# Feed-forward phases: one ring of three PSUM banks for both kinds of centred tiles, a new order in each queue, no loop

## What is computed

```python
def _qlinear(x, W, b):
    y = q_acc(jnp.einsum('bsk,nk->bsn', q_mul(x), q_mul(W)))   # q_mul: fp8 e5m2, q_acc: fp16
    return q_acc(y + q_mul(b))
h = jax.nn.relu(_qlinear(x, W1, b1))      # 24 -> 96
y = _qlinear(h, W2, b2)                   # 96 -> 24
...
t = t + ffn(_ln_t(t), ...)                # _ln_t: (v - mean) / sqrt(var + 1e-5) over channels
x = x + next_mixer(_ln_c(x))              # _ln_c: the same with 1e-6
```

## Time and profile before

| what | value |
|---|---|
| median of three runs | 3313.1 us |
| the profiled execution | 3312.0 us, span 3310.4 us |
| granted TensorE clock, mean | 0.969 |
| TensorE busy | 2831.6 us (86%) |
| VectorE busy | 2666.6 us (81%) |
| ScalarE busy | 2258.8 us (68%) |
| GpSimd busy | 1860.7 us (56%) |
| feed-forward of layer 0 | about 462 to 632 us of the span |
| of layer 1 | 1971 to 2146 us |
| of layer 2 | 2676 to 2851 us |
| of layer 3 (last) | 3165 to 3310 us |

### The profile page before, as it was taken

One profiled execution on the slowest core, in us unless ns is written; L12 is line 12 of the kernel. 1 busy time (PEld: TensorE's weight loads), 2 busy tenths in 40 slices (PEclk: granted clock), 3 DMA queues, 4 the chain that ended last, 5 costly groups with the idle time before them and its releaser, 6 DMA issues. The chain is left out here.

```text
span 3310.4 us, 65685 instructions
## 1 busy us (share of the span) xinstructions
PE 2831.6 (86%) x20846; PEld 1477.4 (45%) x20846; DVE 2666.6 (81%) x4380; ACT 2258.8 (68%) x4205; POOL 1860.7 (56%) x1466
## 2 busy tenths in 40 slices
PE   8999989686999999999997678789999779688876
PEld 5666654233444444444442224344444334477732
DVE  6888879536999999999999958769999968444468
ACT  5666658576999898989895427666777558444455
POOL 2333323155889898989897635447777745100046
PEclk9999999898999999999999999989999989899999
DMA  2000001256474747474746232201101012301023
GB/s 88 0 0 0 0 14 45 81 172 175 120 209 135 221 140 222 140 217 141 217 124 185 59 79 74 76 21 25 24 23 25 18 56 89 126 22 23 22 71 78
DMA packets 201533, 294.28 MB, mean 89 GB/s; under 512 B 62242, under 2 KB 179158, under 8 KB 201110
## 3 DMA queue, kind: packets, MB, share of 16 engines
q1 hardware_dynamic: 198678, 288.03, 30.3%
q10 hardware_dynamic: 2688, 4.29, 0.4%
HBM read 190.11 MB, written 102.09 MB: 88 GB/s over the span
## 5 line engine op out<-in xcount | busy, mean ns | idle before, releaser
L1780 POOL TENSOR_TENSOR mam_hc<-mam_h,mam_cs 128x896 f32<-128x896 f32 x336 | 703.5, 2094 | 173.5 <-DVE mam_h L1699 98.7
L1699 DVE TENSOR_TENSOR_SCAN mam_h<-mam_a,mam_kept,mam_dbx 128x448 f32<-128x448 f32 x672 | 737.7, 1127 | 48.4 <-ACT mam_a L1569 47.4
L1422 PE MATMUL mam_ps_y<-mam_hc,mam_ident 128*128 128x448 f32 x1344 | 570.8, 558 | 124.8 <-POOL mam_hc L1780 124.7
L1569 ACT ACTIVATE mam_a<-mam_ft,mam_a_neg 128x448 f32<-128x448 f32 x672 | 409.5, 657 | 77.1 <-DVE mam_h L1699 76.0
L1422 PEld LDWEIGHTS mam_ps_y<-mam_hc,mam_ident 128*128 128x128 f32 x1344 | 249.8, 193 | 425.4 <-POOL mam_hc L1780 216.2
L1686 DVE TENSOR_TENSOR mam_dbx<-mam_ps_u,mam_bs 128x448 f32<-128x448 f32 x672 | 380.7, 610 | 0.0
L682 POOL TENSOR_TENSOR att_prob<-att_prob,att_share 128x588 f32<-128x588 f32 x128 | 149.0, 1186 | 306.8 <-DVE att_share L974 306.8
L2209 POOL TENSOR_TENSOR scan_ch<-scan_h,scan_cs 128x392 f32<-128x392 f32 x192 | 263.7, 1387 | 56.5 <-DVE scan_h L2150 55.3
L368 POOL MEMSET f_squares_ln<- 128x392 f32 x4 | 1.7, 424 | 362.5 <-POOLq L2283 326.5
L387 POOL CAST f_h<-f_hr 128x392 fp8e5<-128x392 f16 x128 | 65.3, 510 | 234.1 <-DVE f_hr L308 234.1
L2150 DVE TENSOR_TENSOR_SCAN scan_h<-scan_decay_by_column,scan_h,scan_drive_by_column 128x392 f32<-128x392 f32 x112 | 196.8, 1757 | 0.0
(11 more groups left out here) (240 smaller groups left out, 6631.1 us busy)
## 6 DMA issues: line engine op xcount, KB each, us to landing
mam_taps<-normed SPq DMA_DIRECT2D x220, 130.5 KB
mam_bs<-dram_bc SPq DMA_DIRECT2D x56, 448.0 KB, 9.1
mam_cs<-dram_bc SPq DMA_DIRECT2D x56, 448.0 KB, 11.7
normed<-f_staged SPq DMA_DIRECT2D x96, 203.0 KB
mam_ft<-dram_steps SPq DMA_DIRECT2D x42, 448.0 KB, 4.8
f_mixed<-mixed SPq DMA_DIRECT2D x64, 196.0 KB, 2.4
mam_gt<-dram_gs SPq DMA_DIRECT2D x48, 224.0 KB, 2.7
dram_gs<-mam_gs SPq DMA_DIRECT2D x47, 224.0 KB, 2.8
```

Source lines behind the costliest of these rows:

```text
L1422: mm = pe.matmul(ps_y[p % 2][:, 0:MT], ident[:], hc[t % 2][:, i, :], start=False, stop=(t % 8 == 7 and i == 1))
L1569: act.activation(a[t % 3][:, i, :], ft[p % 2][:, 0, :], ACT.Exp, scale=a_neg[:, at:at + 1]).then_inc(decays, 1)
L1699: dve.tensor_tensor_scan(h[:, n % 8, :], a[t % 3][:, i, :], dbx[:, i, 0:MT], kept[:, at:at + 1], ALU.mult, ALU.add).then_inc(scanned, 1)
L1780: pool.tensor_tensor(hc[t % 2][:], h[:, row:row + 2, :], cs[:, 2 * pair:2 * pair + 2, :], ALU.mult).then_inc(weighed, 1)
```

## The change

The three PSUM banks of centred tiles (two for ff, one for norm) become one ring of three; chunk c of either kind uses bank 2c mod 3. The norm of chunk c moves on VectorE from the end of slot c+3 to the middle of slot c+4 (lag 4). VectorE's slot is ordered by source: first the four steps that read PSUM (round_third, quantize, round_result, norm), then the five on SBUF. GpSimd's quantize_third(c) waits also for hidden8(c), that is for VectorE's cast of the same chunk, and its loop becomes quantize_third(c), update(c-1), add_mixed(c+4). TensorE's slot becomes second_product(s-2), subtract_mean(s+1), the norm's subtract_mean(s-3), variance(ff, s+1), hidden_units(s), variance(ln, s-3). ScalarE's becomes round_hidden(s-1), square(ff, s+1), square(ln, s-3), inverse_deviation(ff, s+1), inverse_deviation(ln, s-3). The loops of VectorE, ScalarE and TensorE are written out. SyncE's code does not change.

```diff
-        fronts = [buf.psum(f"xc_ff{p}", [P, BANK]) for p in range(2)]
-        xc_ln = buf.psum("xc_ln", [P, BANK])
+        ring = [buf.psum(f"centred{p}", [P, BANK]) for p in range(3)]
...
-        lag = 3
...
-        def slots(eng, slot):
-            def active(s):
-                return [0 <= s - stage < CHUNKS for stage in (0, 1, 2, lag)]
-            for s in range(3):
-                slot(s, 0, s, active(s))
-            with eng.Fori(0, CHUNKS // UNROLL - 1) as t:
-                for i in range(3, 3 + UNROLL):
-                    slot(t * UNROLL + i, t + i // UNROLL, i % UNROLL, [True] * 4)
-            for s in range(CHUNKS - 1, CHUNKS + 3):
-                slot(s, s // UNROLL, s % UNROLL, active(s))
...
+        lag = 4
+        end = CHUNKS + (2 if last else lag)
+        def bank(c):
+            return ring[2 * c % 3]
+        def is_chunk(c):
+            return 0 <= c < CHUNKS
...
-                    dve.tensor_tensor(xq[:], fronts[u % 2][:, 0:N], rstd["ff"][:], ALU.mult,
+                    dve.tensor_tensor(xq[:], bank(c)[:, 0:N], rstd["ff"][:], ALU.mult,
...
-                def norm(c, turn, u):
+                def norm(c):
                     dve.wait_ge(ln["scaled"], c + 1 + nb)
-                    reached(dve, st.stored[u % 2], (turn * (UNROLL // 2) + (
-                        u // 2 + layer * (CHUNKS // 2))) * 16)
-                    dve.tensor_tensor(staged[u % 2][:, :, 1:SIDE + 1],
-                                      xc_ln[:, 0:N].rearrange("c (r q) -> c r q",
-                                                                        q=SIDE),
+                    reached(dve, st.stored[c % 2], (c // 2 + layer * (CHUNKS // 2)) * 16)
...
+                    dve.tensor_tensor(staged[c % 2][:, :, 1:SIDE + 1],
+                                      bank(c)[:, 0:N].rearrange("c (r q) -> c r q", q=SIDE),
...
-                def slot(s, turn, u, on):
-                    if on[1]:
+                for s in range(end):
+                    if is_chunk(s - 1):
                         round_third(s - 1)
-                    if on[0]:
-                        quantize(s, u)
-                    if on[1]:
+                    if is_chunk(s):
+                        quantize(s)
+                    if is_chunk(s - 2):
+                        round_result(s - 2)
+                    if not last and is_chunk(s - lag):
+                        norm(s - lag)
+                    if is_chunk(s - 1):
                         rectify_third(s - 1)
-                    if on[2]:
-                        round_result(s - 2)
-                    if on[1]:
                         rectify(s - 1, 0)
-                    if on[2]:
+                        rectify(s - 1, 1)
+                    if is_chunk(s - 2):
                         add_bias(s - 2)
-                    if on[1]:
-                        rectify(s - 1, 1)
-                        quantize_hidden(s - 1, (u - 1) % 2)
-                    if not last and on[3]:
-                        norm(s - lag, turn - int(u < lag), (u - lag) % UNROLL)
-                slots(dve, slot)
+                    if is_chunk(s - 1):
+                        quantize_hidden(s - 1)
...
+                    pool.wait_ge(ff["hidden8"], c + 1 + fb)
...
-                quantize_third(0)
-                for c in range(CHUNKS):
-                    if c + 1 < CHUNKS:
-                        quantize_third(c + 1)
-                    update(c)
+                for c in range(CHUNKS + 1):
+                    if is_chunk(c):
+                        quantize_third(c)
+                    if is_chunk(c - 1):
+                        update(c - 1)
                     if c + AHEAD_ADDED < CHUNKS and not in_place:
                         add_mixed(c + AHEAD_ADDED)
...
-                    from_ = fronts[u % 2] if name == "ff" else xc_ln
-                    act.activation(squares[name][:], from_[:, 0:N], ACT.Square
+                    act.activation(squares[name][:], bank(c)[:, 0:N], ACT.Square
...
-                def slot(s, turn, u, on):
-                    if on[0]:
-                        inverse_deviation(ff, "ff", fb, eps_t, "quantized", s)
-                    if on[1]:
+                square(ff, "ff", fb, 0)
+                inverse_deviation(ff, "ff", fb, eps_t, "quantized", 0)
+                for s in range(end):
+                    if is_chunk(s - 1):
                         round_hidden(s - 1)
-                    if not last and on[3]:
-                        square(ln, "ln", nb, s - 3, u)
-                    if has_next(s):
-                        square(ff, "ff", fb, s + 1, u + 1)
-                    if not last and on[3]:
-                        inverse_deviation(ln, "ln", nb, eps_c, "normed", s - lag)
-                square(ff, "ff", fb, 0, 0)
-                slots(act, slot)
+                    if is_chunk(s + 1):
+                        square(ff, "ff", fb, s + 1)
+                    if not last and is_chunk(s - 3):
+                        square(ln, "ln", nb, s - 3)
+                    if is_chunk(s + 1):
+                        inverse_deviation(ff, "ff", fb, eps_t, "quantized", s + 1)
+                    if not last and is_chunk(s - 3):
+                        inverse_deviation(ln, "ln", nb, eps_c, "normed", s - 3)
...
-                def subtract_mean(s, name, base, ready, reader, c, u):
-                    if ready == "updated":
-                        pe.wait_ge(ff["updated"], c + 1 + fb)
-                    elif not in_place:
+                def centre_of(s, c):
+                    pe.matmul(bank(c)[:, 0:N], centre[:], x[:, c * N:(c + 1) * N],
+                              start=True, stop=True).then_inc(s["centred"], 1)
+                def subtract_mean(c):
+                    if not in_place:
                         pe.wait_ge(ff["added"], c + 1 + ab)
-                    held = int(name == "ff")
-                    if base > 0 or not isinstance(c, int) or c > held:
-                        pe.wait_ge(s[reader], c + base - held)
-                    to = fronts[u % 2] if name == "ff" else xc_ln
-                    pe.matmul(to[:, 0:N], centre[:], x[:, bass.ds(c * N, N)],
-                              start=True, stop=True).then_inc(s["centred"], 1)
+                    reached(pe, ff["quantized"], c - 2 + fb)
+                    if not last:
+                        reached(pe, ln["normed"], c - 5 + nb)
+                    centre_of(ff, c)
+                def subtract_mean_again(c):
+                    pe.wait_ge(ff["updated"], c + 1 + fb)
+                    pe.wait_ge(ff["quantized"], min(c + 4, CHUNKS) + fb)
+                    reached(pe, ln["normed"], c - 2 + nb)
+                    centre_of(ln, c)
                 def variance(s, name, base, c):
...
-                def front(c):
-                    subtract_mean(ff, "ff", fb, "added", "quantized", c, c)
-                    variance(ff, "ff", fb, c)
-                def slot(s, turn, u, on):
-                    if on[1]:
-                        hidden_units(s - 1)
-                    if on[2]:
-                        second_product(s - 2, u % 2)
-                    if not last and on[3]:
-                        subtract_mean(ln, "ln", nb, "updated", "normed", s - 3, u)
-                    if has_next(s):
-                        subtract_mean(ff, "ff", fb, "added", "quantized", s + 1, u + 1)
-                    if not last and on[3]:
-                        pe.wait_ge(ff["summed16"], (s - 1 if on[2] else CHUNKS) + fb)
-                        variance(ln, "ln", nb, s - 3)
-                    if has_next(s):
-                        variance(ff, "ff", fb, s + 1)
-                    if isinstance(s, int) and s < 2:
-                        multiply_zeros(2)
-                front(0)
+                subtract_mean(0)
+                variance(ff, "ff", fb, 0)
                 multiply_zeros(2)
                 pe.wait_ge(st.prepared, prep0 + preps)
-                slots(pe, slot)
+                for s in range(end):
+                    if is_chunk(s - 2):
+                        second_product(s - 2)
+                    if is_chunk(s + 1):
+                        subtract_mean(s + 1)
+                    if not last and is_chunk(s - 3):
+                        subtract_mean_again(s - 3)
+                    if is_chunk(s + 1):
+                        variance(ff, "ff", fb, s + 1)
+                    if s < 2:
+                        multiply_zeros(2)
+                    if is_chunk(s):
+                        hidden_units(s)
+                    if not last and is_chunk(s - 3):
+                        pe.wait_ge(ff["summed16"], min(s - 1, CHUNKS) + fb)
+                        variance(ln, "ln", nb, s - 3)
```

More of the change, by code:

```diff
@@ L186, in feed_forward_phase @@
         prep0 = layer * preps
-        lag = 3
-        def slots(eng, slot):
-            def active(s):
-                return [0 <= s - stage < CHUNKS for stage in (0, 1, 2, lag)]
```

(19 more changed lines are left out.)

4 lines of the change are left out of this document (2 added, 2 removed).

## The result

The median of four runs is 3434.2 us (3428.2 to 3438.3), against 3314.6 for the kernel before in the same comparison: a ratio of 1.036, 95% interval 1.034 to 1.039. The forecast was 3438. The profiled execution after took 3434.8 us, span 3433.1, at a mean granted clock of 0.964 (0.969 before). VectorE is busy for 2613.8 us, 53 less than before, and GpSimd for 1833.4, 27 less. TensorE (2832.6, 1 more) and ScalarE (2270.2, 11 more) have about the work that they had. So the added 120 us are almost all idle time, in every queue.

What follows compares the result with a forecast made beforehand. Layers 0 to 2 were taken as bound by the single norm bank's 4.53 us ring, not a busy engine. 6 + 55 + 54 + 11 = 126 on the profiled 3312.0 gave 3438 us; range roughly 3405 to 3468, widened to 3390 to 3475.

Steps and rivals of the forecast that it cites:

- The load ring: Layers 1 and 2: mixed tile's load issued too late, a one-slot ring of 6.8 us; +55 and +54 us.
- the rival of slow landings: Layers 1 and 2: late loads also land slowly, rounds of 7.6 instead of 6.8; +42, 3480 us; chance 0.09.
- Layer 0: TensorE's second_product waits for Ln each slot, 4.59 to 4.9 us: +9, tail about -3, together +6 us.
- The cast: VectorE's cast shortens if GpSimd waits; about 75 us less busy time, hidden in layers 0 to 2.
- If GpSimd waits for the cast: VectorE's queue: under this condition the cast is worth 0.48 us, making 3.32 us a slot; otherwise 3.93.
- The last rival: VectorE's cast isn't shortened by GpSimd's waiting; up to 19 us in the last layer, 3457; chance 0.05.
- The last layer: Late load puts GpSimd's add on VectorE's short steps; 4.25 us a slot taken, 31 x 0.35 = +11 us.
- If it doesn't, the slot is 3.9 as before: Last layer: if GpSimd's add doesn't stop VectorE's short steps, the slot stays 3.9 us; otherwise 4.4.
- Idle some 2 us each: Layers 1 and 2, a sign: GpSimd's mixed-tile adds idle some 2 us each before starting, released by the DMA.
- The first two rivals: Load in time: TensorE's order sets 4.9 us a slot, 3338, chance 0.06; or neither binds, 4.1, 3255, chance 0.05.
- No loop: Written-out streams save branches but need longer programs fetched; taken as 0, between -7 and +5 us.

Runs made afterwards that it cites:

- e1: The changed kernel with the mixed tile's load of chunk c+8, not c+6, issued behind the store of chunk c: 3324.5 us, ratio 1.0037.
- e2: The kernel before the change with the load of chunk c+8 behind the store of c: 3307.4 us, ratio 0.9984.
- e3: The changed kernel with GpSimd's add of the mixed tile one chunk later in its queue, loads unchanged (c+6): 3366.5 us, ratio 1.0167.
- e4: The changed kernel with TensorE's centring product of chunk s+1 ahead of second_product(s-2), loads unchanged: 3434.9 us, ratio 1.0367.
- e5: The changed kernel with the load of chunk c+8 and TensorE's centring product of s+1 ahead of second_product: 3288.2 us, ratio 0.9928.
- e8: The kernel before the change, with GpSimd's cast of the last third made to wait for VectorE's cast of the same chunk: 3328.8 us, ratio 1.0060.
- e7: The changed kernel with the load of chunk c+8 and without GpSimd's wait for VectorE's cast: 3313.4 us, ratio 1.0004.
- e11: The kernel before the change with VectorE's new order alone, norm staying last: 3314.7 us, ratio 1.0018.
- e6: The changed kernel (load of c+6) with second_product(s-2) behind both centring products in TensorE's slot: 3600.1 us in one run.

## Why the prediction was right, and where it was not

**The total.** The forecast was a rise of 126 us, the measured one is 119.6. That 3438 and 3434.2 lie closer than this is chance: the forecast started from an execution of 3312.0, and the kernel before took 3314.6 in the comparison.

**The load ring** (55 + 54): right in mechanism and size. The trace shows the ring, e1 removes it with one constant, e2 shows that the constant gives nothing where there is no ring, e3 breaks it from the other end. The forecast round was 6.8; the quick ones take 6.66, and the 26 together 6.86 (2007.4 to 2185.6) in the mean, because some landings are slower and some rounds have second_product at the low clock. The slowest round, in the table by stretch, behind one at a low clock and a common one:

```profile
2056.78:2063.40 6.62, 5.52 (x18) 2.66 (x17) 3.50 (x13) 3.94 (x7) 2.36 (x3) 0.74 0.21 62
2063.40:2070.06 6.66, 4.08 (x18) 1.95 (x17) 3.58 (x13) 3.94 (x7) 2.35 (x3) 1.00 0.20 61
...
2124.41:2133.01 8.60, 4.30 (x17) 2.10 (x16) 3.57 (x12) 3.94 (x7) 2.35 (x3) 0.94 0.18 50
```

In the slot of 8.60 the load was issued at 2125.74 and the add began at 2130.02, 4.28 later instead of 2.53 (2064.75 to 2067.28). That was the rival of slow landings; it happened in 3 of 26 rounds (3.34, 4.11 and 4.28 from issue to add), not as the rule. Two more rounds of over 7 us (7.16 and 7.27) are another thing: their landings are common ones (2.52 and 2.65), and second_product, at the low clock, took 1.14 instead of 0.66 and brought the next norm 1.69 behind its start instead of 1.21. The Trainium skill's advice (DMA: Bandwidth & Descriptors, Rules for kernel authors) to issue early and wait late held here: e1 issues two chunks earlier and takes back 110 us, e3 waits a slot later and takes back 35 in each of the two layers.

**Layer 0** (+6): measured +6.1, with a slot of 4.98 for 4.9. The two parts were each 1.5 off and cancelled: the 27 steps of 4.98 add 10.5 to the 4.59 of before (forecast +9), and the last four, 13.8 in all, give back 4.6 (forecast 3). e4 and e5 show that the bubble behind Ln is the cause: filling it gives 12.8.

**The cast**: its gain of VectorE's time is hidden, as said, and e8 shows it in the kernel before. The condition "If GpSimd waits for the cast" holds as it stands: in e8 the wait alone brings the mean to 564 ns. What was missed is that the change brings a second cause, sufficient by itself: e7 and e11 get the same short cast with no wait, by the order of VectorE's queue. So the wait is superfluous in the change, and without it the kernel is 11 us faster (e7 against e1). The last rival, a cast that stays at 1.17, did not come true.

**The last layer** (+11): right in sign, mis-sized by a factor of two: +5.5, that is 126.3 / 31 = 4.07 a slot for 4.25. The term had two parts. What the late load costs is right: after against e1 it is 126.3 - 115.6 = 10.7. What was wrong is the base, "If it doesn't, the slot is 3.9 as before": with the load in time a slot takes 115.6 / 31 = 3.73, and 106.0 / 31 = 3.42 without the wait for the cast as well. The likely reason is VectorE's shorter cast, which I had booked as hidden everywhere: in this layer, which has no norm ring, VectorE is busy for 111.8 of 121 us before and for 98.7 of 106 in e7. That is argued and not shown. No run separates the cast from the rest of the new order here, and in the kernel before, e8 and e11 shorten the cast and make this layer longer. The Trainium skill (SBUF — State Buffer, Who interferes with whom) says that tensor_scalar steps of VectorE in a two-port mode, such as rectify, and GpSimd's instructions exclude each other for a whole instruction. The pair of short steps at 3362.93, 1.30 us beside GpSimd's add, agrees.

**"Idle some 2 us each"** for GpSimd's adds was wrong: 4.31 in the slot shown, and 118.2 / 26 = 4.5 in the mean of the ring's 26 adds in layer 1. The ring's sum didn't rest on it: GpSimd's other work of a slot, 0.51 and 0.93 beside the add's 1.01, leaves 6.66 - 2.45 = 4.2 idle, which could have been worked out beforehand.

**The first two rivals** (the load in time, with or without a bubble) fall with e1. What they promised is what one gets when the cause is taken away: e1 has 148 to 152 us in layers 0 to 2, near the first one's 4.9 a slot, and e5 135.5, 4.37 a slot, for the second one's 4.1.

**No loop** (0) was never priced by itself: no run changes the loops alone. The 3 us between the sum by phase (116.5) and the medians (119.6) leave little room for it outside the stretches measured.

**The range.** Added up at their ends, the parts named give 3399 to 3477 and not 3405 to 3468; the measured time lies in both.

## What to carry to other kernels

When a step is moved by a slot, write down for every transfer how many slots lie between the step that lets it be issued and the step that wants it, in both kernels; where the step that lets the load be issued comes too late for it to land in time, the latency becomes part of a ring and each slot pays all of it; here that was a threshold and no slope. A change that consists of several parts is priced part by part: here the new structure, once its load came in time and TensorE's order was mended, was worth 7 to 9 us a norm phase, and two side effects had buried it. Where two engines hold each other up, the order in one queue can decide which of them is held, without a wait; either way, look for who stands behind the one that is held now.

## What was not expected of the hardware

- Which engine is held when VectorE's cast and GpSimd's add meet depends on who starts first: cast 1.17 and add 0.94 with the add 0.2 ahead, cast 0.56 and add 1.19 with the cast 0.15 ahead (e7). From the first start to the last end the pair takes the same, 1.37 and 1.34: nothing is saved, it is only decided which queue pays.
- After a wait of 2.58 us in e6 the four passes of the centring product took 3.02 us at a granted clock of 0.51, and in the kernel after, where TensorE had waited about as long (2.56, ahead of second_product at 2068.85), they took 1.48 at 1.00. The wait's length alone doesn't say which it will be. In a ring that is bound by a DMA the lower clock is free where the slow products aren't in it: the slots at 0.74 and 1.00 above take 6.62 and 6.66. Where second_product is hit, it costs 0.48 a round (the slots of 7.16 and 7.27).
